# The activation of a gated MLP turned by VectorE and DRAM instead of TensorE, with part of the down projection moved into the next tile

## Chip, cores and metric

One core of a Trainium2 chip runs the kernel. The metric is the device time of one execution in microseconds (us). Before the change three runs gave 551.83 us as median (549.92 to 553.22).

## What is computed

x is 64 x 32 x 512. First comes a long convolution per channel (32 channels, 512 positions) with a mask by length, then a gated MLP with one LoRA adapter per batch element; both are added to x. What the change touches is the second step:

```
gate = lora_add(einsum('bnh,fh->bnf', x, W_gate), x, A_gate, B_gate)
up   = lora_add(einsum('bnh,fh->bnf', x, W_up),   x, A_up,   B_up)
act  = silu(gate) * up                      # F = 1376 columns
down = lora_add(einsum('bnf,hf->bnh', act, W_down), act, A_down, B_down)
x    = x + down
```

lora_add adds 0.5 * (inp @ A[idx].T) @ B[idx].T, with idx chosen per batch element (`itok_B_2_6`). H is 512, the rank 16.

## The kernel before

The first 80 us build the convolution's taps and do the convolution of 16 pairs of channels. The MLP then runs over 16 tiles of 128 rows (4 batch elements x 32 rows), `tiles(...)`: tile 0 alone, a loop of 7 rounds with two tiles each, tile 15 alone. Each engine runs its own `body(a, q, first, last)` with t = 2a + q; semaphores order the engines, and within an engine the order is the one written.

Weights stay in SBUF as pairs, `w_hi`/`w_lo` and `wd_hi`/`wd_lo`, and each product is three matmuls (hi x hi, lo x hi, hi x lo), so that the 32-bit result keeps its digits. The 1376 columns of gate and up are three chunks `CH` of 512, 512 and 352 columns; `BLK` counts them in blocks of 128: 4, 4 and 3 (the last has 96 rows).

TensorE per tile: `base(c, up)` multiplies x by the weights of chunk c (12 matmuls) into `ps_g` or `ps_u`, `lora(c, up)` adds two LoRA matmuls. ScalarE takes SiLU of `ps_g` into `h_act`, VectorE multiplies by `ps_u` (`gated`). The down projection needs the activation with its columns on the partitions, so `transpose_act(c)` (L1035) turns each block of `h_act` on TensorE, against the identity, into `ps_x`. ScalarE casts that into `ht_hi`, VectorE subtracts into `ht_lo` (`ht_hi_part`, `ht_lo_part`), and `down_chunk(c)` (L1044) accumulates in `ps_da` (288 columns) and `ps_db` (224 columns of the output and 64 of the LoRA A product). Chunk 2 is written out at the end of the body, `ps_db` first, since td_m needs it. `lora_a(t)` (L986) makes the next tile's LoRA A product. The LoRA part of the down projection (`transpose_td`, `down_lora`) comes inside the next tile, and so does `finish`, which adds the residual.

SyncE issues every DMA, in one queue: `load_b` (B of a chunk, four issues), `load_a`, `load_bd`, `store` of the output, and index reads ahead of them. The residual itself already takes the road that the change uses for the activation: `square_x` (L816) transposes 32x32 blocks on VectorE into `x_sq`, `store_x` (L324) writes it to the DRAM tensor `xrow` in four issues, one for each 32 partitions, and `load_y` (L328) reads it back turned. `b_raw` are two tiles of 64 partitions; `b_hi_part` and `b_lo_part` (L494, L822) split it into the halves of `b_spl`. GpSimd's `body` (L429, L410) copies the next tile's x and A once A has landed.

## Time and profile before

| | |
|---|---|
| median of three runs | 551.83 us |
| the profiled execution | 551.96 us |
| its span on the core | 550.2 us |
| granted TensorE clock | 0.992 of full |
| TensorE matmul busy | 514.0 us (93%) |
| VectorE busy | 265.1 us (48%) |
| ScalarE busy | 190.9 us (35%) |
| GpSimd busy | 39.2 us (7%) |
| DMA engines, the one queue of SyncE | 39.3% |

Busy time is the sum of an engine's instructions; the span runs from the first to the last record. The time of the execution is 1.8 us longer than its span. Of the views named below, the chain follows the last instruction back to what released it; the timeline lists instructions in order; SPq is SyncE's queue, whose entries are the issues of DMAs and not the transfers.

### The profile page before, as it was taken

To read this page: it belongs to the slowest core of one execution; us is meant where nothing else is said; L and a number is where in the kernel's file an instruction comes from. 1 tells how busy PE (TensorE), PEld (TensorE's weight loads), DVE (VectorE), ACT (ScalarE), POOL (GpSimd) and SP (SyncE) were. 2 spreads that over 40 slices of the span, in tenths; PEclk is the share of its full clock that TensorE was granted. 3 is DMA by queue.
4 is the path that set the end of the run, shared out by engine and by line. 5 is a ranking of instruction groups with operands and counts; after the bars stand their busy time and mean duration, and the time that the engine had idled before them with its cause. 6 is when DMAs were issued, how large, how long until landed. Compare 5 with 4: busy or idle time off the path is not lost.

```text
span 550.2 us, 10109 instructions
## 1 busy us (share of the span) xinstructions
PE 514.0 (93%) x3105; PEld 467.3 (85%) x3105; DVE 265.1 (48%) x572; ACT 190.9 (35%) x411; POOL 39.2 (7%) x55
## 2 busy tenths in 40 slices
PE   0198889999999999999999999999999999999997
PEld 0097787989898989999898989898989898999986
DVE  7882266754444435353445453444444443525342
ACT  6790007333333333242324232323333333324221
POOL 1006700100000000000000000000000000000000
PEclk9998899999999999999999999999999999999999
DMA  7899993423142323242323232322324132423200
GB/s 277 287 344 390 312 331 72 101 71 94 48 108 43 112 51 112 51 112 51 112 48 105 55 97 60 82 67 75 84 51 106 43 110 49 112 51 112 52 21 19
DMA packets 68403, 61.59 MB, mean 112 GB/s; under 512 B 41634, under 2 KB 50242, under 8 KB 68386
## 3 DMA queue, kind: packets, MB, share of 16 engines
q1 hardware_dynamic: 68386, 61.39, 39.3%
q8 instruction: 8, 0.13, 0.1%
q14 instruction: 9, 0.07, 0.0%
HBM read 52.89 MB, written 8.47 MB: 112 GB/s over the span
## 4 chain that ended last, share of the span: by engine, by line
PE 86%; DVE 5%; DMA 5%; ACT 1%; issue 1%; SPq 0%; DVEq 0%
PE ps_g L1006 21%; PE ps_u L1006 21%; PE ps_db L1044 13%; PE ps_da L1044 13%; PE ps_x L1035 3%; PE ps_x L986 3%; PE ps_g L960 3%; DMA toep<-kpad 2%; DMA kpad<-k_sb 2%; PE ps_u L960 2%; PE ps_g L1016 2%; PE ps_u L1016 2%; PE ps_g L1017 2%; PE ps_u L1017 2%; PE ps_da L1104 1%
## 5 line engine op out<-in xcount | busy, mean ns | idle before, releaser
L494 ACT CAST b_spl<-b_raw 64x512 fp32r<-64x512 f32 (+1 forms) x96 | 54.4, 569 | 98.3 <-PE ps_u L1017 78.9
L822 DVE TENSOR_TENSOR b_spl<-b_raw,b_spl 64x512 fp32r<-64x512 f32 (+1 forms) x96 | 60.7, 633 | 53.8 <-ACT b_spl L494 50.1
L1006 PE MATMUL ps_g<-w_hi,x_hi 128*128 128x512 f32 (+1 forms) x192 | 72.7, 379 | 1.4 <-DVE x_lo L917 1.4
L1006 PE MATMUL ps_u<-w_hi,x_hi 128*128 128x512 f32 (+1 forms) x192 | 71.4, 372 | 0.0
L1006 PE MATMUL ps_u<-w_lo,x_hi 128*128 128x512 f32 (+1 forms) x192 | 71.3, 371 | 0.0
L1006 PE MATMUL ps_u<-w_hi,x_lo 128*128 128x512 f32 (+1 forms) x192 | 71.3, 371 | 0.0
L1006 PE MATMUL ps_g<-w_lo,x_hi 128*128 128x512 f32 (+1 forms) x192 | 71.1, 370 | 0.0
L1006 PE MATMUL ps_g<-w_hi,x_lo 128*128 128x512 f32 (+1 forms) x192 | 71.0, 370 | 0.0
L858 DVE TENSOR_TENSOR h_act<-h_act,ps_u 128x512 f32<-128x512 f32 (+1 forms) x48 | 30.3, 632 | 53.7 <-PE ps_u L1017 53.6
L1044 PE MATMUL ps_da<-wd_hi,ht_hi 128*128 128x288 f32 (+1 forms) x176 | 54.5, 310 | 0.2 <-DVE ht_lo L865 0.2
L1044 PE MATMUL ps_db<-wd_hi,ht_hi 128*128 128x288 f32 (+1 forms) x176 | 53.3, 303 | 0.0
L1044 PE MATMUL ps_db<-wd_hi,ht_lo 128*128 128x288 f32 (+1 forms) x176 | 52.1, 296 | 0.0
L1044 PE MATMUL ps_db<-wd_lo,ht_hi 128*128 128x288 f32 (+1 forms) x176 | 52.0, 295 | 0.0
L1044 PE MATMUL ps_da<-wd_lo,ht_hi 128*128 128x288 f32 (+1 forms) x176 | 51.9, 295 | 0.0
L1044 PE MATMUL ps_da<-wd_hi,ht_lo 128*128 128x288 f32 (+1 forms) x176 | 51.7, 294 | 0.0
L517 ACT ACTIVATE h_act<-ps_g 128x512 f32<-128x512 f32 (+1 forms) x48 | 26.5, 552 | 63.8 <-PE ps_g L1017 63.8
L1006 PEld LDWEIGHTS ps_u<-w_hi,x_lo 128*128 128x128 f32 x192 | 36.1, 188 | 5.8
L1006 PEld LDWEIGHTS ps_u<-w_hi,x_hi 128*128 128x128 f32 x192 | 36.1, 188 | 5.7
L1006 PEld LDWEIGHTS ps_g<-w_hi,x_hi 128*128 128x128 f32 x192 | 36.1, 188 | 5.7 <-issue 1.5
L1006 PEld LDWEIGHTS ps_u<-w_lo,x_hi 128*128 128x128 f32 x192 | 36.1, 188 | 5.7
L1006 PEld LDWEIGHTS ps_g<-w_hi,x_lo 128*128 128x128 f32 x192 | 36.0, 188 | 5.7
L1006 PEld LDWEIGHTS ps_g<-w_lo,x_hi 128*128 128x128 f32 x192 | 36.2, 188 | 4.4
(165 smaller groups left out, 871.3 us busy)
## 6 DMA issues: line engine op xcount, KB each, us to landing
a_raw<-atab SPq DMA_DIRECT2D x64, 152.0 KB, 2.4
toep<-kpad SPq DMA_DIRECT2D x16, 512.0 KB, 7.5
b_raw<-btab SPq DMA_DIRECT2D x128, 64.0 KB, 2.0
um<-xr SPq DMA_DIRECT2D x16, 256.0 KB, 5.5
x<-xT SPq DMA_DIRECT2D x8, 512.0 KB, 6.9
w_raw<-wgu SPq DMA_DIRECT2D x8, 512.0 KB, 9.3
xrow<-x_sq SPq DMA_DIRECT2D x64, 64.0 KB, 2.2
y_sb<-xrow SPq DMA_DIRECT2D x16, 256.0 KB, 2.6
```

Of the source, the lines that this page charges most:

```text
L494: nc.scalar.copy(b_spl[0:LR, up, 0:w], b_raw[slot][:, up * w:(up + 1) * w]).then_inc(b_hi, 1)
L517: nc.scalar.activation(h_act[:, s, 0:w], ps_g[s][:, 0:w], ACT.Silu).then_inc(silu_ok, 1)
L822: V.tensor_tensor(b_spl[LR:P, up, 0:w], b_raw[slot][:, up * w:(up + 1) * w], b_spl[0:LR, up, 0:w].bitcast(F32), ALU.subtract).then_inc(b_l ...
L858: V.tensor_tensor(h_act[:, s, 0:w], h_act[:, s, 0:w], ps_u[s][:, 0:w], ALU.mult).then_inc(act_ok, 1)
L960: last = T.matmul(ps_c[slot][:, at + d * NB:at + KB * NB], toep[:, slot, h, d * P:(d + 1) * P], v, start=(d == 0), stop=(d == KB - 1))
L986: ins = T.matmul(ps_x[0][:, 0:P], w, xt[:, kb, :], start=(kb == 0), stop=(kb == KB - 1))
L1006: T.matmul(ps[:, 0:w], xs[:, kb, :], ws[:, kb, col:col + w], start=(kb == 0 and xs is x_hi and ws is w_hi), stop=False)
L1016: T.matmul(ps[:, 0:w], t_hi[:, up, :], b_spl[:, up, 0:w], start=False, stop=False)
L1017: T.matmul(ps[:, 0:w], t_lo[:, up, :], b_spl[:, up, 0:w], start=False, stop=True).then_inc(u_ps if up else g_ps, 1)
L1035: ins = T.transpose(ps_x[bank][0:rows, f * P:(f + 1) * P], h_act[:, s, f * P:f * P + rows], ident[:, :])
L1044: ins = T.matmul(ps[:, 0:c1 - c0], hs[0:rows, f, :], ws[0:rows, f, c0:c1], start=(f == 0 and hs is ht_hi and ws is wd_hi), stop=(bank == 1 ...
L1104: T.matmul(ps_da[:, 0:DA_W], ts[:, :], bd_spl[:, 0:DA_W], start=False, stop=end)
```

## The change

Three things are changed.

- `transpose_act` is gone. `square_h(c)` transposes the 32x32 blocks of `h_act` on VectorE, into a new tile `h_sq` for chunks 0 and 2 and into `x_sq` for chunk 1. `store_h` writes it to a DRAM tensor `hrow` with four issues per chunk, `load_h` reads it back turned into `h_raw` (two tiles; chunk 2 has two issues, since its last block has 96 rows). `ht_hi_part` and `ht_lo_part` now read `h_raw` in SBUF instead of `ps_x`.
- On TensorE only down chunk 0 stays at the end of the tile. `down_rest(t)` does chunks 1 and 2 behind the first gate group of the next tile; in tile 15 it follows at once.
- The orders of SyncE, ScalarE and VectorE follow from that. `load_a` of the next tile comes before the output store. `h_act` has one slot where it had two; the two `b_raw` tiles are now the halves of one tile of 128 partitions, and the halves of `b_spl` swap with them. `lora(0, 0)` comes behind `base(0, 1)` and `down_lora` behind `base(1, 0)`.

```diff
@@ sync
+            def store_h(t, c):
+                col, w = CH[c]
+                sp.wait_ge(hsq_ok, NC * t + c + 1)
+                for part in range(P // Q):
+                    rows = x_sq if c == 1 else h_sq
+                    src = rows[part * Q:(part + 1) * Q, 0:w].rearrange("q (f t) -> q f t", t=Q)
+                    into = bass.AP(tensor=hrow, offset=col * P + part * Q, ap=[[P, Q], [Q * P, w // Q], [1, Q]])
+                    sp.dma_start(into, src).then_inc(h_out, 16)
+
+            def load_h(t, c):
+                f0, nf = BLK[c]
+                full = nf if c < NC - 1 else nf - 1
+                sp.wait_ge(h_out, 16 * (P // Q) * (NC * t + c + 1))
+                src = bass.AP(tensor=hrow, offset=f0 * P * P, ap=[[P, P], [P * P, full], [1, P]])
+                sp.dma_start(h_raw[c % 2][:, 0:full, :], src).then_inc(h_in[c], 16)
...
                 if not last:
                     ids = indices(na, nq)
+                    load_a(na, nq, ids)
+                store_h(t, 0)
+                if not last:
                     load_b(na, nq, 0, ids)
                 if not first:
                     store(*((a, 0) if q == 1 else (a - 1, 1)))
+                load_h(t, 0)
                 if not last:
-                    load_a(na, nq, ids)
                     load_bd(na, nq, ids)
+                store_h(t, 1)
+                if not last:
                     load_b(na, nq, 1, ids)
+                load_h(t, 1)
+                store_h(t, 2)
+                if not last:
                     store_x(t + 1)
+                load_h(t, 2)
+                if not last:
                     load_y(t + 1, nq)
@@ scalar
-                    td_hi_part(t - 1)
+                    ht_hi_part(t - 1, 2)
...
-                    wait(act, ht_ps, n - 1)
+                    wait(act, hsq_ok, n)
...
-                ht_hi_part(0)
+                ht_hi_part(t, 0)
                 silu(2)
                 if not last:
+                    x_hi_part(na, nq, False)
                     b_hi_part(na, nq, 0, 0)
                     b_hi_part(na, nq, 0, 1)
-                ht_hi_part(1)
-                if not last:
-                    x_hi_part(na, nq, False)
-                ht_hi_part(2)
+                ht_hi_part(t, 1)
+                if last:
+                    ht_hi_part(t, 2)
@@ vector
-                    td_lo_part(t - 1)
+                    ht_lo_part(t - 1, 2)
+                    td_m_part(t - 1)
...
+                def square_h(c):
+                    n = NC * t + c
+                    dve.wait_ge(act_ok, n + 1)
+                    if c == 1:
+                        dve.wait_ge(xrow_out, 16 * (P // Q) * (t + 1))
+                    else:
+                        wait(dve, h_out, 16 * (P // Q) * (n - c // 2))
+                        wait(dve, htlo_ok, (NC + 1) * t + c // 2)
+                    V.transpose((x_sq if c == 1 else h_sq)[:, 0:CH[c][1]], h_act[:, 0:CH[c][1]]).then_inc(hsq_ok, 1)
...
+                if not first:
+                    td_lo_part(t - 1)
+                gated(0)
+                square_h(0)
                 b_lo_part(a, q, 1, 0)
-                gated(0)
@@ tensor
+            def down_rest(t):
+                pe.wait_ge(htlo_ok, (NC + 1) * t + 2)
+                down_chunk(1)
+                pe.wait_ge(htlo_ok, (NC + 1) * (t + 1))
+                for f in range(BLK[2][0], FB):
+                    ins = down(f, 1)
+                ins.then_inc(ad_ps, 1)
+                for f in range(BLK[2][0], FB):
+                    ins = down(f, 0)
+                ins.then_inc(down_ps, 1)
...
-                transpose_act(1)
-
-                pe.wait_ge(htlo_ok, (NC + 1) * t + 1)
...
+                pe.wait_ge(htlo_ok, (NC + 1) * t + 1)
                 down_chunk(0)
-                transpose_act(2)
-                pe.wait_ge(htlo_ok, (NC + 1) * t + 2)
-                down_chunk(1)
-                if not last:
+                if last:
+                    down_rest(t)
+                else:
                     lora_a(t + 1)
```

Where instructions move is shown at three places, all in the tile of the loop with q = 1. TensorE before, from the end of down chunk 1 of a tile (ps_da and ps_db) through the LoRA A product to chunk 2:

```order
457 L1044 MATMUL ps_db<-wd_hi,ht_lo 128x288
458 L981 REGISTER_ALU
459 L982 REGISTER_ALU [waits ag_ok]
460 L986 MATMUL ps_x<-xt,a_gu 128x128 [waits htlo_ok,xt_ok]
461 L986 MATMUL ps_x<-xt,a_gu 128x128 x3
462 L1087 REGISTER_ALU
463 L1044 MATMUL ps_db<-wd_hi,ht_hi 128x288 [waits htlo_ok]
```

TensorE after, behind down chunk 0; the first gate group of the next tile (425 to 436) stands ahead of down chunk 1 (438 on):

```order
418 L1042 MATMUL ps_db<-wd_hi,ht_lo 128x288
419 L1029 REGISTER_ALU
420 L1030 REGISTER_ALU [waits ag_ok]
421 L1034 MATMUL ps_x<-xt,a_gu 128x128 [waits tm_ok,xt_ok]
422 L1034 MATMUL ps_x<-xt,a_gu 128x128 x3
423 L1075 ISA
424 L192 ISA [waits xlo_ok]
425 L1080 MATMUL ps_g<-w_hi,x_hi 128x512 [waits act_ok]
...
436 L1080 MATMUL ps_g<-w_hi,x_lo 128x512
437 L1053 ISA
438 L1042 MATMUL ps_da<-wd_hi,ht_hi 128x288 [waits htlo_ok]
```

Down chunks 1 and 2 moved behind twelve matmuls of the next tile, and no transpose stands between them. SyncE's queue before, at the end of a tile, from B's last issue to the residual:

```order
213 L311 DMA b_raw<-btab 16x1024
214 L320 REGISTER_ALU
215 L324 DMA xrow<-x_sq 128x4x32 [waits xsq_ok]
216 L324 DMA xrow<-x_sq 128x4x32 x3
217 L327 REGISTER_ALU
218 L328 DMA y_sb<-xrow 128x512 [waits xrow_out]
```

SyncE's queue after, at the same place:

```order
230 L318 DMA b_raw<-btab 16x1024
231 L369 REGISTER_ALU
232 L371 DMA h_raw<-hrow 128x4x128 [waits h_out]
233 L359 REGISTER_ALU
234 L364 DMA hrow<-h_sq 32x11x32 [waits hsq_ok]
235 L364 DMA hrow<-h_sq 32x11x32 x3
236 L327 REGISTER_ALU
237 L331 DMA xrow<-x_sq 128x4x32 [waits xsq_ok]
238 L331 DMA xrow<-x_sq 128x4x32 x3
239 L369 REGISTER_ALU
240 L371 DMA h_raw<-hrow 128x2x128 [waits h_out]
241 L373 DMA h_raw<-hrow 96x128
```

The load of chunk 1, four stores of chunk 2 and its two load issues are new here; the load of chunk 2 stands behind all four stores of xrow. VectorE after, from the gating of chunk 0 on:

```order
180 L908 TENSOR_TENSOR h_act<-h_act,ps_u 128x512 [waits u_ps,silu_ok]
181 L192 REGISTER_ALU [waits act_ok]
182 L918 STREAM_TRANSPOSE h_sq<-h_act 128x512 [waits htlo_ok,h_out]
183 L853 ISA
184 L854 TENSOR_TENSOR b_spl<-b_raw,b_spl 64x512 [waits b_hi]
185 L853 REGISTER_ALU
186 L854 TENSOR_TENSOR b_spl<-b_raw,b_spl 64x512 [waits b_hi]
187 L864 ISA [waits y_ps]
```

and before, at the same place:

```order
177 L821 ISA
178 L822 TENSOR_TENSOR b_spl<-b_raw,b_spl 64x512 [waits b_hi]
179 L858 TENSOR_TENSOR h_act<-h_act,ps_u 128x512 [waits u_ps,silu_ok]
180 L821 REGISTER_ALU
181 L822 TENSOR_TENSOR b_spl<-b_raw,b_spl 64x512 [waits b_hi]
182 L832 ISA [waits y_ps]
183 L833 TENSOR_TENSOR y_sb<-y_sb,ps_da 128x288 [waits y_in]
184 L834 TENSOR_TENSOR y_sb<-y_sb,ps_db 128x224
```

The gating stood between the two splits of B; now it and the transpose stand ahead of both.

## Rows read from the trace of the kernel before

**Rows 1.** The page: busy us, share and instructions of each engine; the chain by engine.

```profile
PE 514.0 (93%) x3105; PEld 467.3 (85%) x3105; DVE 265.1 (48%) x572; ACT 190.9 (35%) x411; POOL 39.2 (7%) x55
...
PE 86%; DVE 5%; DMA 5%; ACT 1%; issue 1%; SPq 0%; DVEq 0%
```

**Rows 2.** The chain in order of time, one tile: start us, us, what.

```profile
343.54 2.79 PE ps_g L1006 x12
346.90 2.80 PE ps_u L1006 x12
350.64 2.80 PE ps_g L1006 x12
...
357.15 0.44 PE ps_x L1035 x4
...
359.83 1.92 PE ps_u L1006 x12
362.08 0.44 PE ps_x L1035 x4
369.23 0.89 PE ps_x L986 x8
...
372.52 2.79 PE ps_g L1006 x12
```

**Rows 3.** Timeline of TensorE, chunk 2's transposes: start, us, engine, line, what.

```profile
336.56 0.49 PE L1035 MATMUL ps_x<-ident,h_act 128*128 128x128 f32 x3
...
337.02 0.29 PE L1044 MATMUL ps_da<-wd_lo,ht_hi 128*128 128x288 f32 x1
```

**Rows 4.** SyncE's queue: its timeline over one tile, and the second index reads.

```profile
311.73 0.35 SPq L328 DMA_DIRECT2D y_sb<-xrow  x1
314.65 1.85 SPq L311 DMA_DIRECT2D b_raw<-btab  x4
...
322.86 1.81 SPq L311 DMA_DIRECT2D b_raw<-btab  x4
324.95 0.38 SPq L333 DMA_DIRECT2D out<-y_sb  x1
325.56 1.91 SPq L270 DMA_DIRECT2D a_raw<-atab  x4
327.65 1.84 SPq L317 DMA_DIRECT2D bd_raw<-btab  x4
...
336.44 2.64 SPq L324 DMA_DIRECT2D xrow<-x_sq  x4
...
L262 SPq FUSED_REGOPS  x8: 46/106/152, 316.5 to 318.8; - x8
```

**Rows 5.** Issue durations (ns, min/median/max) of two lines; landings of xrow's and y_sb's transfers.

```profile
L247 SPq DMA_DIRECT2D kpad<-k_sb x4: 326/341/971, 20.5 to 42.3; - x4
...
L253 SPq DMA_DIRECT2D toep<-kpad x16: 377/384/469, 22.1 to 69.8; - x16
...
xrow<-x_sq SPq DMA_DIRECT2D x64, 64.0 KB, 2.2
...
DMA to landing us min/median/max: 2.6/2.6/2.8
```

The last line is that of y_sb<-xrow (L328), the one before gives KB and the median landing.

**Rows 6.** VectorE's block transpose, and the two splits of the turned chunk 2.

```profile
L816 DVE STREAM_TRANSPOSE x_sq<-xt x16: 704/704/709, 80.1 to 509.6; 128x512 f32<-128x512 f32 x16
...
337.08 0.37 ACT L529 CAST ht_hi<-ps_x 128x256 fp32r<-128x256 f32 x1 [2.33 <-PE ps_x L1035]
...
337.99 0.28 DVE L869 TENSOR_TENSOR ht_lo<-ps_x,ht_hi 96x128 fp32r<-96x128 f32 x1
```

**Rows 7.** Timeline of TensorE in tile 0, down chunk 0.

```profile
101.38 0.40 PE L1044 MATMUL ps_da<-wd_hi,ht_hi 128*128 128x288 f32 x1 [0.22 <-DVE ht_lo L865]
```

**Rows 8.** Timeline of the last tile: VectorE's gating of chunk 1, TensorE's down chunk 2.

```profile
531.18 0.69 DVE L858 TENSOR_TENSOR h_act<-h_act,ps_u 128x512 f32<-128x512 f32 x1 [1.81 <-PE ps_u L1017]
...
542.99 0.29 PE L1044 MATMUL ps_db<-wd_hi,ht_hi 128*128 128x288 f32 x1
```

176 lines of the change are left out of this document (77 added, 99 removed).

## The prediction

> **What bounds the kernel now.** I read the busy shares first: TensorE is busy for 93% of the span and carries 86% of the chain that ended last [rows 1]; VectorE, ScalarE and the DMA engines are busy less than half of it. The second view is the chain in order of time. From the first gate product of one tile to that of the next it is TensorE alone, 372.52 - 343.54 = 28.98 us, and nothing in it is a wait [rows 2]; sixteen such tiles are 464 of the 550 us. So in the middle tiles every instruction taken off TensorE shortens the kernel by its own length, as long as no other engine or queue then comes last. The third view is SyncE's queue [rows 4], because the change puts its new transfers there: whether the gain arrives is decided on that queue.
>
> **What is removed.** Eleven transposes per tile on TensorE. Four are 0.44 us in the chain, twice (357.15 and 362.08) [rows 2]. The three of chunk 2 stand between 336.56 and 337.02 [rows 3]: the start of the second matmul behind them comes 0.46 us after their own, of which 0.13 is the pitch of one 288-column matmul (18 of them fill the 2.40 from 370.12 to 372.52 in the chain), so 0.33. Sum 1.21 us per tile. TensorE's own work becomes 28.98 - 1.21 = 27.8 us.
>
> **What is added, and what covers it.** I count from the moment Z at which the up projection of chunk 0 is complete. Behind it come on TensorE the lengths of [rows 2]: 2.8 (chunk 1's gate), 0.48 (the LoRA part of the down projection of the tile before) and 0.46 (one LoRA pair; both together are the 0.94 between 346.90 + 2.80 and 350.64), 2.8, 0.46 and 2 x (1.92 + 0.32) for chunk 2 (359.83 to 362.08 is 2.25). Chunk 1 is therefore complete at Z + 7.0 and chunk 2 at Z + 11.5. Then follow down chunk 0 (24 matmuls at 0.133 = 3.2), the LoRA A product (0.89 at 369.23), the next tile's first gate group (2.8), down chunk 1 (3.2) and down chunk 2 (2.4, from 370.12 to 372.52). So the turned chunk 0 is needed at Z + 11.3, chunk 1 at Z + 18.2, chunk 2 at Z + 21.4.
>
> The new road of a chunk is: gating multiply (0.69 at 531.18 [rows 8]; about 0.5 for chunk 2's 352 columns), 32x32 block transpose, four stores to DRAM, a load back, the cast on ScalarE and the subtraction on VectorE. The transpose exists: 0.704 us for 128x512 [rows 6]; for 352 columns I scale it to 0.5. VectorE and ScalarE are idle for half the time, so these add no length by themselves, only latency. A store issued as xrow's lands 2.2 us after its issue, a load as y_sb's 2.6 (2.8 at most) [rows 5].
>
> The unknown is the time that SyncE needs to issue one hrow store; the trace has two rows for it. xrow's store takes 0.66 us with its gap (2.64 for four [rows 4]). kpad's takes 0.341 (median of four) [rows 5]. They differ in kind: xrow's store walks its tile as 32x16x32 and DRAM as 128x4x32, while kpad's has one shape on both sides, 32x8x16, and toep's load with one shape, 128x2x512, is issued in 0.384. The hrow store is 32x16x32 on both sides. I take 0.38 with its gap, and keep 0.66 as the other end. A load of h_raw I put at 0.4.
>
> SyncE's order behind Z, with the lengths of [rows 4]: hrow store of chunk 0 from Z + 1.7 (gating and transpose end there), 1.5; B of the next tile 2.0; the output store 0.6; load of chunk 0 0.4; bd 2.1; this is Z + 8.3, the square of chunk 1 is there at Z + 8.6; store 1.5, B 2.0, load 0.4: Z + 12.5, the square of chunk 2 is there at Z + 12.7; store 1.5 (Z + 14.2); xrow's four stores 2.65 (Z + 16.9); load of chunk 2, two issues, the second from Z + 17.3.
>
> - Chunk 0: load issued at Z + 5.8, landed 8.4, ScalarE 0.6 and VectorE 0.7: Z + 9.8, needed at 11.3. Margin 1.5 us.
> - Chunk 1: load at Z + 12.1, landed 14.7, behind it ScalarE's and VectorE's turn (VectorE has the next tile's x and B ahead of it until 15.5): Z + 16.6, needed at 18.2. Margin 1.6 us.
> - Chunk 2: landed at Z + 19.3 to 19.9; from the first ScalarE cast to the end of the last subtraction 1.2 us (337.08 to 338.27 [rows 6]): Z + 20.6 to 21.2, needed at 21.4. **Margin 0.2 to 0.8 us**, the thinnest of the three.
>
> SyncE's own round must also fit in 27.8 us. Behind the load of chunk 2: 0.9 waiting for xrow to land, 0.36 for y_sb, 0.3 for the loop, the first four index reads 2.6 (312.08 to 314.65), B of chunk 2 1.85, the second four 2.5 (from 316.5), A 2.1 [rows 4]. Together 10.6, plus 15.4 from the list above: 26.0 us. It fits, with 1.8 to spare. The A load is no longer behind the output store; it waits for the subtraction of wd_lo, which comes some 2 us ahead of Z, so it starts at Z - 1.6 and is out at Z + 0.5, ahead of the first hrow store at 1.7. GpSimd waits only for that A load, and now gets it earlier.
>
> A new order costs nothing at two more places. VectorE now gates and transposes chunk 0 before chunk 1's first B split: the split is ready at Z + 2.4, TensorE wants it at Z + 3.1. The single h_act tile makes the next SiLU wait for the transpose, which is done at 1.7 where the next SiLU comes at about 3.9.
>
> **The two ends.** In tile 0 VectorE is loaded with weight remainders, and TensorE already waits there for ht_lo (101.38) [rows 7]. The transpose of chunk 0 (0.7, ahead of the split) and that of chunk 1 (0.7, ahead of the last remainders) push both, so TensorE starts down chunk 0 at about 102.25 and not 101.38; of the tile's transposes only the last 0.33 come off behind that point. Tile 0: +0.5. In the last tile no next gate group covers the road. Chunk 1: gated from 531.18 [rows 8], square ready at 532.6, stores to 534.2, landed 536.05, load landed 538.8, ready 540.1, while TensorE is there at 538.6: 1.6 us. Chunk 2: its store follows the load of chunk 1 (536.8), landed 540.1, load landed 542.7, ready 544.1; TensorE, at 543.3 by then, loses 0.8. Down chunk 2 began at 542.99 [rows 8] and now begins at about 544.2: +1.2 net of the transposes.
>
> **Sum.** Against the profiled run's own 551.96 (span 550.2 and 1.8 around it; the three plain runs have a median of 551.83, so the two agree): 14 middle tiles x 1.21 = -16.9, tile 0 +0.5, last tile +1.2. 551.96 - 15.2 = 536.8 us.
>
> **Rivals.**
> 1. *SyncE's queue becomes the bound, and the kernel is slower.* If the hrow store is issued at xrow's 0.66, twelve of them cost 3.4 us more per tile. The load of chunk 2 then ends at Z + 20.5 and not 17.1, and the ring closes: behind that last issue landing, cast, subtraction and down chunk 2 take 5.7 us, then 3.8 us of TensorE to the next Z and 1.7 to the next hrow store, 11.2 in all, plus 18.8 of issues: 30.0 us per tile against 28.98. 14 x 1.06 + 3 at the ends gives 570 us; with chunk 2's 11-block stores at 11/16 of the price 29.2 and 558. It decides from a mean of about 0.57 per store on (a tile of 28.98); below about 0.45 TensorE stays the bound. For it: xrow's row is the only one with as many 128-byte runs (512). Against: the equal shapes. The Trainium skill (DMA: Bandwidth & Descriptors, "Issuing engines are not separate DMA queues") calls issue time "usually small relative to the DMA itself", which speaks against this rival; the trace does not agree, four xrow issues (2.64 us) are longer than one landing (2.2).
> 2. *The round trip of chunk 2 is later than its margin.* Behind xrow's stores and beside B and A loads the landing may be 0.5 to 1 us longer than 2.6. Each us beyond the margin is 14 us of kernel: 0.5 gives 544, 1.0 gives 551. For it: the margin of 0.2 to 0.8. Against: all sixteen landings of y_sb, which are issued right behind xrow's stores, are between 2.6 and 2.8 [rows 5]. The Trainium skill (VectorE: DVE Perf Modes, "The three transpose paths") warns of a transpose by strided plain copy as 19 times slower where the innermost destination stride is large, and sends 128x128 blocks to TensorE. Its condition is not met here, the innermost run is 32 contiguous floats, and xrow's row, turned the same way, shows 2.2 us for 64 KB.
> 3. *No change.* A price of 0.54 to 0.6 per store gives back just what the transposes gave: 549 to 555.
>
> **Chances.** Forecast (TensorE stays the bound, 533 to 541) 0.62; rival 2, 541 to 549, 0.15; rival 3 and the mild half of it, 549 to 555, 0.07; rival 1, 0.12; below 533, 0.04. The range takes the forecast and rival 2: 533 to 550. This kernel's measurement tells 0.5% from no change; by that bound faster has 0.80, same 0.07, slower 0.13.
>
> **What would show it.** Right: the first gate products of two tiles 27.8 us apart, no wait of TensorE for ht_lo in the middle tiles, hrow<-h_sq at about 0.34 us per issue, SyncE waiting for VectorE's square once or twice per tile. Wrong: hrow stores at 0.6 us and TensorE waiting at the first matmul of down chunk 2 in every tile (rival 1), or that wait with cheap issues and landings of 3 us and more (rival 2). A wait at chunk 1 or 0, or at B's first split, would say that my order of VectorE's work is wrong.

## The result, and the profile after

The changed kernel is slower: 576.56 us (median of 6 runs, 574.11 to 580.70) against 551.53 (6 runs, 549.92 to 553.22), a ratio of 1.046 (95% interval 1.042 to 1.050). The prediction was 536.8, faster. The profiled execution took 580.7 us with a span of 578.9, against 551.96 and 550.2. It is the longest of the six.

The page of the changed kernel: the busy lines answer to the first of [rows 1], the chain line to the second.

```profile
PE 510.6 (88%) x2929; PEld 458.5 (79%) x2929; DVE 297.4 (51%) x620; ACT 196.5 (34%) x411; POOL 43.3 (7%) x55
...
SPq 42%; PE 25%; DMA 12%; issue 10%; DVE 8%; ACT 3%; DVEq 0%
SPq L364 15%; SPq L318 9%; PE ps_u L1080 8%; SPq L331 7%; DMA h_raw<-hrow 6%; PE ps_db L1042 4%; SPq L324 4%; PE ps_da L1042 4%; SPq L371 4%; PE ps_g L1008 3%; DMA toep<-kpad 2%; PE ps_u L1008 2%; DVE h_sq L918 2%; DVE h_act L908 2%; DMA kp
```

The 176 transposes are gone (3105 to 2929 matmuls), yet TensorE's share of the chain fell from 86% to 25%, and SyncE's queue has 42%, with the hrow stores (L364) first. The next view is the list of waits (engine, line, releaser: us in total, times, longest us).

```profile
PE ps_db L1042 <- DVE ht_lo L875: 23.9, 15, 2.1
...
PE ps_da L1042 <- DVE ht_lo L872: 6.9, 5, 4.2
```

TensorE waits in each of the 15 tiles that have a predecessor, for the last piece of the chunk 2 before it, 1.6 us on average, and one wait of 4.2 us, for chunk 0, lies in tile 0. A middle tile in SyncE's timeline, then what follows it on ScalarE, VectorE and TensorE (start us, us, engine, line, what); the rows of before are [rows 4].

```profile
342.55 1.97 SPq L364 DMA_DIRECT2D hrow<-h_sq  x4
344.80 1.85 SPq L318 DMA_DIRECT2D b_raw<-btab  x4
346.95 0.38 SPq L340 DMA_DIRECT2D out<-y_sb  x1
347.47 0.39 SPq L371 DMA_DIRECT2D h_raw<-hrow  x1
348.13 1.86 SPq L324 DMA_DIRECT2D bd_raw<-btab  x4
350.03 2.05 SPq L364 DMA_DIRECT2D hrow<-x_sq  x4
352.36 1.85 SPq L318 DMA_DIRECT2D b_raw<-btab  x4
354.32 0.39 SPq L371 DMA_DIRECT2D h_raw<-hrow  x1
354.82 2.02 SPq L364 DMA_DIRECT2D hrow<-h_sq  x4
356.95 2.65 SPq L331 DMA_DIRECT2D xrow<-x_sq  x4
359.72 0.55 SPq L371 DMA_DIRECT2D h_raw<-hrow  x1
360.31 0.48 SPq L373 DMA_DIRECT2D h_raw<-hrow  x1
```

```profile
362.73 0.40 ACT L540 CAST ht_hi<-h_raw 128x256 fp32r<-128x256 f32 x1 [2.26 <-DMA h_raw<-hrow]
...
363.70 0.28 DVE L875 TENSOR_TENSOR ht_lo<-h_raw,ht_hi 96x128 fp32r<-96x128 f32 x1
...
364.04 0.40 PE L1042 MATMUL ps_db<-wd_hi,ht_hi 128*128 128x288 f32 x1 [1.67 <-DVE ht_lo L875]
```

Chunk 0's up projection is complete at Z = 340.83 here. The first hrow store goes out at Z + 1.7, as predicted; the second h_raw issue of chunk 2 at Z + 19.5 instead of 17.3. TensorE stands at Z + 21.6 (predicted 21.4) and gets the data at Z + 23.2.

A second thing was in no part of the prediction. The windows around that wait (us; busy us of PE, PEld, DVE, ACT, POOL; granted clock, DMA share, GB/s):

```profile
339.50:362.40 22.90, 22.87 (x134) 20.49 (x132) 13.17 (x25) 8.54 (x18) 1.38 (x2) 1.00 0.64 141
362.40:364.04 1.64, 0.00 (x1) 0.00 (x1) 0.62 (x2) 0.60 (x2) 0.00 (x0) 1.00 0.43 145
364.04:365.50 1.46, 1.46 (x11) 1.46 (x12) 0.00 (x0) 0.00 (x0) 0.00 (x0) 1.00 0.00 0
365.50:367.50 2.00, 2.00 (x11) 2.00 (x10) 0.29 (x1) 0.00 (x0) 0.00 (x0) 0.51 0.33 76
367.50:369.50 2.00, 2.00 (x8) 1.55 (x7) 0.89 (x1) 0.78 (x1) 0.00 (x0) 0.64 0.04 14
```

TensorE stood still for 1.64 us, worked for 1.5, and then had a granted clock of 0.51, its lower level of 1.2 GHz, for some 3 us, though it was busy all the time. Five of the 14 middle tiles have a mean clock of 0.95 and last 31.35 us or more; the others, at 1.00, last 29.39 to 29.75. In the kernel before, every tile shows 1.00. The number of such tiles differs between executions: the profiled one has a mean granted clock of 0.978, four of the other five have 0.984. One stretch at 0.50 for some 3 us lowers the mean over 579 us by about 0.003, so by this estimate those four had about two stretches fewer.

**Where the 43.9 us between predicted and measured span went** (535.0 and 578.9), by the starts of the transposes of td (one per tile; 28.99 apart in the kernel before): the first comes at 124.32, 7.8 us later than in a kernel with only the moved down projection (experiment 1), where I had 0.5 for the tile (7.3 us); the next 14 steps take 426.3 us instead of 14 x 27.82 = 389.5 (36.8 us, of which 14 x 1.79 = 25.1 is the step of 29.61, the mean of the nine ordinary tiles, and 11.7 the rest of the five longer tiles with their low clock; the first two of them, at 33.0 and 32.5, also have longer and further waits); the last tile is 0.9 us longer, 0.3 less than predicted.

### The profile page after: what moved, and what is told of

It reads as the page before. It is cut to its first block, busy times and chain, and to the rows that moved or that the text cites. A ratio compares the mean times of both kernels' runs of the same rounds, so it can differ in the third digit from the quotient of the medians.

```text
span 578.9 us, 10207 instructions
## 1 busy us (share of the span) xinstructions
PE 510.6 (88%) x2929; PEld 458.5 (79%) x2929; DVE 297.4 (51%) x620; ACT 196.5 (34%) x411; POOL 43.3 (7%) x55
## 2 busy tenths in 40 slices
DMA packets 182579, 84.15 MB, mean 145 GB/s; under 512 B 133794, under 2 KB 164418, under 8 KB 182562
## 4 chain that ended last, share of the span: by engine, by line
SPq 42%; PE 25%; DMA 12%; issue 10%; DVE 8%; ACT 3%; DVEq 0%
SPq L364 15%; SPq L318 9%; PE ps_u L1080 8%; SPq L331 7%; DMA h_raw<-hrow 6%; PE ps_db L1042 4%; SPq L324 4%; PE ps_da L1042 4%; SPq L371 4%; PE ps_g L1008 3%; DMA toep<-kpad 2%; PE ps_u L1008 2%; DVE h_sq L918 2%; DVE h_act L908 2%; DMA kpad<-k_sb 2%
## 5 line engine op out<-in xcount | busy, mean ns | idle before, releaser
L1042 PE MATMUL ps_db<-wd_hi,ht_hi 128*128 128x288 f32 (+1 forms) x176 | 54.5, 310 | 23.9 <-DVE ht_lo L875 23.9
L1080 PE MATMUL ps_u<-w_hi,x_hi 128*128 128x512 f32 (+1 forms) x192 | 72.7, 378 | 0.0
L540 ACT CAST ht_hi<-h_raw 128x512 fp32r<-128x512 f32 (+1 forms) x48 | 26.3, 548 | 135.8 <-DMA h_raw<-hrow 135.8
L872 DVE TENSOR_TENSOR ht_lo<-h_raw,ht_hi 128x512 fp32r<-128x512 f32 (+1 forms) x48 | 29.0, 603 | 81.6 <-ACT ht_hi L540 51.0
L528 ACT CAST b_spl<-b_raw 64x512 fp32r<-64x512 f32 (+1 forms) x96 | 51.7, 571 | 53.3 <-PE ps_u L1091 33.6
L1042 PEld LDWEIGHTS ps_db<-wd_hi,ht_hi 128*128 128x128 f32 (+1 forms) x176 | 33.6, 191 | 27.7 <-DVE ht_lo L875 27.7
L1042 PE MATMUL ps_da<-wd_hi,ht_lo 128*128 128x288 f32 (+1 forms) x176 | 53.9, 306 | 0.0
L1042 PE MATMUL ps_da<-wd_lo,ht_hi 128*128 128x288 f32 (+1 forms) x176 | 53.9, 306 | 0.0
L463 POOL COPY xt<-x 128x512 f32 (+1 forms) x15 | 11.5, 766 | 435.9 <-DMA a_raw<-atab 435.9
L1042 PEld LDWEIGHTS ps_da<-wd_hi,ht_hi 128*128 128x128 f32 (+1 forms) x176 | 35.0, 199 | 9.9 <-DVE ht_lo L872 4.7
```

What stands on the lines that cost most here:

```text
L528: nc.scalar.copy(b_spl[b_rows(slot), up, 0:w], b_raw[b_rows(slot), up * w:(up + 1) * w]).then_inc(b_hi, 1)
L540: nc.scalar.copy(ht_hi[:, f0:f0 + full, :], raw[:, 0:full, :]).then_inc(hthi_ok, 1)
L872: V.tensor_tensor(ht_lo[:, f0:f0 + full, :], raw[:, 0:full, :], ht_hi[:, f0:f0 + full, :].bitcast(F32), ALU.subtract).then_inc(htlo_ok, 1)
L1042: ins = T.matmul(ps[:, 0:c1 - c0], hs[0:rows, f, :], ws[0:rows, f, c0:c1], start=(f == 0 and hs is ht_hi and ws is wd_hi), stop=(bank == 1 ...
L1080: T.matmul(ps[:, 0:w], xs[:, kb, :], ws[:, kb, col:col + w], start=(kb == 0 and xs is x_hi and ws is w_hi), stop=False)
```

## The experiments

Each ratio is against executions of the kernel before that belong to the same experiment; "step" is the mean distance of two td transposes over the 14 middle tiles of the profiled execution.

| | kernel | median us | ratio (95%) | step us |
|---|---|---|---|---|
| | before | 551.53 | | 28.99 |
| | after | 576.56 | 1.046 (1.042 to 1.050) | 30.45 |
| 1 | move only | 551.87 | 1.000 (0.998 to 1.003) | 29.03 |
| 2 | traffic only | 558.04 | 1.012 (1.007 to 1.016) | 29.25 |
| 3 | stall, 5 transposes | 552.79 | 1.003 (1.000 to 1.005) | 28.99 |
| 5 | stall, 8 transposes | 586.33 | 1.063 (1.060 to 1.067) | 31.12 |
| 4 | xrow from ScalarE | 566.68 | 1.028 (1.023 to 1.033) | 29.67 |
| 6 | xrow behind h_raw | 571.80 | 1.038 (1.035 to 1.042) | 30.08 |
| 13 | xrow in blocks | 560.64 | 1.017 (1.015 to 1.018) | 29.15 |
| 14 | hrow from ScalarE | 555.22 | 1.009 (1.005 to 1.012) | 28.94 |
| 7 | tile 0's order | 575.83 | 1.043 (1.038 to 1.047) | 30.36 |
| 8 | reordered | 551.04 | 1.000 (0.998 to 1.003) | 28.77 |
| 9 | round shortened | 550.71 | 0.999 (0.997 to 1.001) | 28.61 |
| 10 | 9, xrow in blocks | 551.38 | 1.001 (0.998 to 1.004) | 28.77 |
| 11 | h_raw 0 before a | 569.51 | 1.033 (1.030 to 1.036) | 29.98 |
| 12 | 11, tile 0 changed | 570.48 | 1.034 (1.032 to 1.037) | 30.11 |
| 15 | third order | 557.97 | 1.012 (1.008 to 1.016) | 29.23 |
| 16 | 15, bd last | 540.09 | 0.981 (0.978 to 0.983) | 28.06 |

### The two parts of the change apart (1, 2)

```diff
@@ tensor, on the kernel before (1)
                 base(0, 0)
-                if not first:
-                    transpose_td(t - 1)
+                down_rest(t - 1)        # chunks 1 and 2
+                base(0, 1)
+                transpose_td(t - 1)
...
                 transpose_act(2)
-                pe.wait_ge(htlo_ok, (NC + 1) * t + 2)
-                down_chunk(1)
@@ sync, on the kernel before (2)
+                store_h(t, 0)           # source: w_lo, a constant tile
...
+                load_h(t, 0)            # nobody reads h_raw
```

> The kernel before with the second part of the change alone: the activation is still turned by TensorE (11 transposes per tile), and only the down projection of chunks 1 and 2 moves behind the next tile's first gate group. Nothing goes through DRAM. Theory A (the ring: SyncE's issues between the first hrow store and chunk 2's h_raw load, the landing and the casts decide when chunk 2's rows are ready, TensorE waits 1.7 us for them in every tile, and the clock falls behind some of those waits): without the round trip nothing is late, TensorE keeps its 28.99 us per tile, total 549 to 554 us. Rival B (the new order on TensorE, with silu and the gating product further apart, is itself what costs): 1 us or more per tile, 565 us or more.

> The kernel before, with the changed kernel's DMA work added and used by nobody: the same 12 hrow stores and 4 h_raw loads per tile on SyncE in the changed kernel's order, the stores taking their data from a constant tile instead of the turned activation (so hrow holds nothing of use); b_raw's two slots lie in one tile, as in the changed kernel, to make room. The products are still computed from TensorE's own transposes. Theory A: the traffic (84 MB instead of 62) costs TensorE nothing by itself, since no TensorE instruction waits for it; SyncE is busy in 28 us of a tile and TensorE's loads have slack, so 550 to 556 us. Rival C (SyncE's issue time or the DMA engines are the bound: a, b or y arrive late): 29.5 us per tile or more, 560 us or more, with TensorE waiting for b_spl or for lora_a's operands.

The move alone costs nothing that shows in the total; it is 29.03 us per tile against 28.99, with no wait. Rival B falls. With the traffic alone (84.15 MB instead of 61.59) TensorE's busy time and clock stay at those of before, 511.8 us and 1.00, and eight of the 14 steps are 28.97 to 29.01 us; but the total is 1.2% up, more than theory A allowed. The profiled execution, at 555.18 us, is the fastest of four (the others took 557.8 to 559.2), so the profile shows only a part of this. The largest part that it shows is one tile of 30.87 us:

```profile
193.72 0.55 PE L1074 MATMUL ps_x<-ident,h_act 128*128 128x128 f32 x3 [1.69 <-DVE ht_lo L904]
```

That wait is of the experiment's own making: so that the unused tile is not written twice at a time, ScalarE waits for h_raw's landing before the third SiLU, up to 5.2 us. So 1.2% holds the cost of the traffic and of this added wait together, and how it divides was not measured. `load_a` stands here behind the load of chunk 0, as it does not in the changed kernel.

### A wait on TensorE without the traffic (3, 5)

```diff
@@ vector, on the kernel before
+                for _i in range(NPAD):        # 5 in run 3, 8 in run 5
+                    V.transpose(pad_sq[:, :], w_lo[:, 0, 0:512])
                 ht_lo_part(2)
```

> The kernel before with five added VectorE square transposes of a constant tile (0.7 us each, one waiting for the other, some 4.5 us) ahead of chunk 2's ht_lo, which TensorE waits for; nothing of the computation is left out. In the profile of before that ht_lo is ready 2.5 us before TensorE wants it, so TensorE should wait about 2.0 us per tile at the down projection of chunk 2, with no added DMA. Theory A on the clock (a wait of this length on TensorE is enough for stretches at half clock to follow): windows of the trace with the granted clock well below 1.00 right behind some of the waits, and a total above 551.5 + 16 x 2.0 = 583 us by some microseconds. Rival D (the half clock of the changed kernel comes from its DMA traffic or its longer run, not from the wait): granted clock 1.00 all through the tiles as in before, total 580 to 585 us.

> The kernel before with eight added VectorE square transposes of a constant tile ahead of chunk 2's ht_lo instead of the five of the last stall run, whose 3.65 us ended 0.4 us before TensorE wanted the result and made no wait; nothing of the computation is left out. Three more at 0.73 us put chunk 2's ht_lo 1.7 to 1.9 us behind TensorE's wish in each of 16 tiles, with no added DMA: about the wait of the changed kernel. Theory A on the clock (such a wait is enough for stretches at half clock to follow behind some of them): granted clock well below 1.00 in windows behind some waits, tiles of 32 us or more among those of 30.8, total 585 us or more. Rival D (the half clock of the changed kernel comes with its DMA traffic): clock 1.00 all through, every tile 30.7 to 30.9 us, total 578 to 582 us.

Five transposes missed their purpose: 3.65 us of them filled a gap of VectorE and the margin behind it, and TensorE never waited. Eight made a wait of 1.65 us, the size of that in the changed kernel. Twelve of the 14 steps are 30.88 to 30.91 us, two are 32.44 and 32.45, with a mean clock of 0.95. The timeline and the windows of one of these two:

```profile
455.95 0.40 PE L1053 MATMUL ps_db<-wd_hi,ht_hi 128*128 128x288 f32 x1 [1.65 <-DVE ht_lo L875]
...
450.00:455.00 5.00, 4.30 (x34) 4.11 (x32) 4.76 (x8) 0.53 (x2) 0.00 (x0) 1.00 0.36 59
...
457.00:459.00 2.00, 2.00 (x13) 2.00 (x12) 0.49 (x2) 0.94 (x4) 0.00 (x0) 0.64 0.27 66
459.00:461.00 2.00, 2.00 (x7) 1.61 (x7) 1.15 (x4) 0.24 (x1) 0.00 (x0) 0.50 0.11 24
```

The same fall to the lower level comes behind a wait, with no hrow traffic at all: rival D falls, and theory A holds. The extra price is 1.55 us per tile that is hit, and about the same in the changed kernel: its three shorter hit tiles take 31.35 to 31.54 us against 29.61, 1.7 to 1.9 more, of which their longer waits (1.67 to 1.89 us against 1.52) are 0.15 to 0.37. Why two tiles are hit here and five in the changed kernel is not explained by these runs.

### What sets the wait for chunk 2: SyncE's issues or the landing (4, 6, 13, 14)

```diff
@@ changed kernel (4): scalar
                     b_hi_part(na, nq, 0, 1)
+                    store_x(t + 1)          # on ScalarE's queue, gone from SyncE
                 ht_hi_part(t, 1)
@@ changed kernel (6): sync
-                    store_x(t + 1)
                 load_h(t, 2)
+                    store_x(t + 1)          # load_y in the next tile, behind load_a
@@ changed kernel (13): store_x
-                    src = x_sq[...].rearrange("q (k j p) -> q k j p", p=Q, k=KB)
+                    src = x_sq[...].rearrange("q (f p) -> q f p", p=Q)
@@ changed kernel (14): scalar
                 b_hi_part(a, q, 1, 1)
+                store_h(t, 0)               # 1 ahead of ht_hi_part(t, 0), 2 behind the next b
```

> The changed kernel with the next tile's four xrow stores (2.65 us of issuing per tile) given to ScalarE's queue, behind its b_spl casts, where it idles from 354.06 to 357.51; all else as in the changed kernel. Theory A (ring): chunk 2's h_raw loads are issued about 2.2 us earlier after the first hrow store of the tile, the rows are ready just before TensorE wants them (362.4 in the tile shown), the wait is gone and with it the half clock: 27.8 to 28.2 us per tile, total 538 to 548 us, tile 0 still about 9 us late. Rival E (the stores of two engines go through the same hardware and slow each other, or the landing gets longer): the hrow burst of chunk 2 takes over 3 us instead of 2.0 and the wait stays, 570 us or more.

> The changed kernel with the xrow stores behind chunk 2's h_raw load on SyncE (y_sb's load then stands in the next tile behind load_a); all on SyncE as before. The run with xrow on ScalarE's queue had shown the same distance from chunk 2's first hrow store to its h_raw load as the changed kernel (4.86 and 4.90 us) though SyncE had nothing to issue in between: what takes that time would be the landing of hrow beside the xrow packets, not SyncE. Theory F (the landing of hrow, 1.8 to 2.0 us alone and some 3.2 beside an xrow burst, is the term): h_raw is issued 3.8 to 4.1 us after the first hrow store of chunk 2, the wait at chunk 2 falls from 1.67 to 0.7 to 0.9, 28.7 to 28.9 us per tile, total 553 to 565 us with less of the half clock. Rival G (the landing of hrow takes 3 us there with or without xrow beside it): the distance stays 4.6 or more and the total 570 us or more. Rival H (SyncE has no room at the tile's end: the xrow stores push the next tile's b and a loads and its first hrow store): the first hrow store comes 1 us or more behind its square, and the gain is given back.

> The changed kernel with xrow kept in hrow's block layout (one shape on both sides of the store), y_sb read back block by block; nothing else. The four xrow issues between chunk 2's hrow stores and its h_raw load then take some 2.0 us instead of 2.65. Issue theory (the prediction's way of adding: the ring is the sum of SyncE's issues): chunk 2's h_raw load comes 0.65 us earlier after its first hrow store (4.25 instead of 4.90 us), the wait falls by 0.65, total 563 to 567 us with fewer stretches at half clock. Landing theory F (the distance is hrow's landing, 3.2 us beside xrow's packets against 1.4 to 1.5 when nothing follows): the distance stays at 4.6 to 4.9 and the total within 3 us of the changed kernel's 576.5.

> The changed kernel with the hrow stores of all three chunks issued by ScalarE (chunk 0 behind b_spl's casts, chunk 1 ahead of chunk 0's ht_hi, chunk 2 behind the next b_spl casts), h_raw, xrow and all else still on SyncE in the same order. SyncE's round falls by 6 us. Issue theory: 27.8 to 28.2 us per tile, total 540 to 550 us. Landing theory F, with ScalarE in order as a rival of its own: ScalarE waits for each square before it goes on (chunk 1's square is done 8 us after the up projection of chunk 0, and silu of chunk 2 stands behind the burst of 2 us), so chunk 0's and chunk 1's casts get later while chunk 2's hrow still lands beside xrow's packets: a wait of 0.5 to 1.5 us per tile stays, total 555 to 575 us.

The measure is the distance from chunk 2's first hrow store to its h_raw load in SyncE's timeline. It is 4.90 us in the changed kernel (354.82 to 359.72 above). Runs 4, 6 and 13, in this order:

```profile
346.72 2.95 ACTq L537 DMA_DIRECT2D xrow<-x_sq  x4
346.76 2.08 SPq L364 DMA_DIRECT2D hrow<-h_sq  x4
351.62 0.38 SPq L371 DMA_DIRECT2D h_raw<-hrow  x1
```

```profile
348.65 1.98 SPq L364 DMA_DIRECT2D hrow<-h_sq  x4
352.04 0.38 SPq L371 DMA_DIRECT2D h_raw<-hrow  x1
```

```profile
312.67 2.02 SPq L365 DMA_DIRECT2D hrow<-h_sq  x4
314.79 2.04 SPq L331 DMA_DIRECT2D xrow<-x_sq  x4
316.95 0.44 SPq L372 DMA_DIRECT2D h_raw<-hrow  x1
```

- Run 13 takes 0.6 us off the four xrow issues (2.65 to 2.04); y_sb is read back block by block, behind chunk 2's load, and nothing else changes. The distance falls to 4.28, the wait from 1.52 us on average in the ordinary tiles to 0.84 in those behind the first three, the total by 16 us. The issue theory had 4.25 for the distance. Its total of 563 to 567 was too high: besides 14 times the shorter wait, tile 0 is 3.7 us shorter (first td transpose at 120.62) and no tile has the low clock. Theory F, as I had put it after run 4, falls: with all stores on one queue the last issue sets the time.
- Run 6 has nothing between the two: 3.39 us, that is 1.4 us of landing behind the end of the burst. Run 4 has nothing between them on SyncE either, but ScalarE's queue issues xrow at the same moment: 4.86 us, 2.8 behind the burst. The landing of hrow doubles beside another queue's stores, and it takes back what the freed SyncE gave at this place. TensorE's wait still falls, to 0.7 to 1.0 us in most tiles, since the h_raw loads of chunk 2 are landed 2.3 to 2.5 us after the first of the two issues, against 2.6 to 3.0 in the changed kernel. Run 4's total, 566.68 us, lies between both its theories. The Trainium skill (DMA: Bandwidth & Descriptors, "Issuing engines are not separate DMA queues") says that transfers issued by different engines run on the same 16 DMA engines and interleave. The trace agrees: 2.8 us behind the burst against 1.4.
- In run 6 the wait for chunk 2 is all but gone (0.17 us), and rival H has come: the first hrow store of a tile goes out at 306.42 though its square ended at 304.17. SyncE had no 2.65 us to give at the tile's end, and TensorE waits 2.44 us for chunk 0 instead in this tile, 0 to 2.3 us in the other middle tiles.
- Run 14 frees SyncE of 6 us per tile and gets 28.94, not 27.8. ScalarE is in order: its cast of chunk 0 stands behind its own burst for chunk 1.

```profile
332.77 1.95 ACTq L528 DMA_DIRECT2D hrow<-x_sq  x4
334.89 0.62 ACT L536 CAST ht_hi<-h_raw 128x512 fp32r<-128x512 f32 x1 [3.26 <-issue]
```

The chunk had landed at 333.24. TensorE then waits 0.7 to 0.9 us for chunk 0 in every middle tile. The bound moved to the engine that took the issues.

### Tile 0 (7)

```diff
@@ changed kernel, sync, tile 0 alone
+                    store_h(t, 0)
                     ids = indices(na, nq)
+                    load_h(t, 0)
                     load_a(na, nq, ids)
-                    store_h(t, 0)
```

> The changed kernel with another order of SyncE's issues in tile 0 alone: chunk 0's hrow stores ahead of the index reads and of load_a, chunk 1's ahead of the next tile's b. In the changed kernel tile 0's first hrow store is issued at 97.36 though its square is done at 92.86, and TensorE waits 4.24 us for chunk 0's ht_lo at 106.39. Theory A: the store goes out near 93, ht_lo of chunk 0 is ready about 5 us earlier, the first transpose of td is at 117 to 119 instead of 124.3, the later tiles are unchanged at 29.6, total 567 to 572 us. Rival: VectorE's and ScalarE's preparation of the weights sets tile 0's end (they hold the casts of wd between the squares), under 2 us is gained, 574 us or more.

The store does go out at 90.66 and the wait for chunk 0 falls from 4.24 to 1.22 us, but a new one of 5.55 us stands at chunk 2, whose h_raw load is issued only at 112.85, behind the next tile's b and xrow. First td transpose at 124.00 against 124.32: nothing gained, neither theory's number. In run 16 only bd's issues stand in tile 0 between chunk 2's hrow stores and its load, xrow is on ScalarE's queue, and the transpose is at 116.53.

### Reordering until no wait is left (8 to 12, 15, 16)

Run 8 takes xrow to ScalarE's queue behind chunk 2's casts, in the next tile, where no hrow is under way, and puts hrow and h_raw of chunks 1 and 2 directly one behind the other. The later runs change SyncE's order, and the index reads as said below:

```diff
@@ sync, a middle tile, b of chunk 2 and the index reads ahead of it
-8:  a, y_sb, hrow 0, b, out, h_raw 0, bd, hrow 1, h_raw 1, hrow 2, h_raw 2, b
+9:  hrow 0, a, h_raw 0, b, out, hrow 1, y_sb, bd, h_raw 1, hrow 2, h_raw 2, b
+11: hrow 0, h_raw 0, a, b, hrow 1, out, y_sb, bd, h_raw 1, hrow 2, h_raw 2, b
+15: hrow 0, h_raw 0, a, y_sb, out, hrow 1, b, h_raw 1, hrow 2, bd, h_raw 2, b
+16: hrow 0, y_sb, out, h_raw 0, a, hrow 1, b, h_raw 1, hrow 2, h_raw 2, bd, b
```

Run 9 also reads a tile's indices once instead of twice in every second tile; 11 to 16 keep that. Run 10 is 9 with xrow in blocks, run 12 is 11 with one VectorE pair swapped in tile 0.

> The changed kernel with all of it put right that the traces point to: the xrow stores on ScalarE's queue in the next tile behind chunk 2's casts (y_sb's load behind load_a), on SyncE hrow and h_raw of chunks 1 and 2 directly one behind the other and the next b after them, and tile 0 with its hrow stores first. Theory F: hrow of chunk 2 goes out about 1.2 us earlier and lands alone; its rows are ready within 0.3 us of TensorE's wish, 27.8 to 28.1 us per tile, tile 0 about 2 to 4 us behind that of before, granted clock 1.00: total 532 to 542 us. Rival G (the landings stay at 3 us): a wait of 0.5 to 1 us per tile, 28.4 to 28.8, total 545 to 553 us. Rival I (the half clock has a cause of its own): tiles of over 30 us remain though no wait is left.

> The reordered kernel of the last call with SyncE's round put right: the first hrow store of a tile goes ahead of load_a and y_sb's load (there it went out at 352.60 behind a_raw at 350.07, 0.95 us behind the end of its square at 351.65), the h_raw load of chunk 0 ahead of the next b, and the indices of a tile are read once instead of twice in every second tile and in tile 0 (a read of four takes some 2.4 us of SyncE's time). Theory J (in the reordered kernel SyncE's round of some 28.8 us is the bound, so that every second tile waits at chunk 0): no wait is left in the later tiles, 27.8 to 28.0 us per tile, total 535 to 542 us. Rival K (what is left is landing time: chunk 0's hrow and h_raw come late beside the a and b loads whatever the order): 28.4 us per tile or more, 546 us or more.

> The last kernel with xrow kept in hrow's layout (blocks of 128 tokens by 128 columns, so that the two sides of a store have one shape) and y_sb read back block by block; the xrow store then reads as the hrow stores do, some 0.50 us each instead of 0.66 to 0.74 on ScalarE's queue. Theory J: nothing on the path, since ScalarE's burst lies where nobody waits: within 1.5 us of the last kernel. Rival: y_sb's load in pieces of 512 bytes lengthens the landings beside it, 2 us or more slower.

> The kernel with the shortened round, with chunk 0's h_raw load put ahead of load_a (SyncE then waits some 1.5 us for hrow's landing), and the out store and y_sb's load behind chunk 1's hrow stores. In the last kernel the h_raw load of chunk 0 was issued at 354.54 behind a_raw's four and its rows reached ScalarE only at 358.73, 4.2 us later against 2.0 alone, and TensorE waited up to 0.67 us for chunk 0. Theory L (a landing is as long as the bytes issued just before it make it): the landing of chunk 0's h_raw falls to 2.0 to 2.6 us, no wait is left at chunk 0, 28.05 to 28.2 us per tile (that is 29.03 less the 0.96 us that TensorE's transposes really took), total 541 to 546 us. Rival M (SyncE's wait for the landing costs its round: chunk 1 or 2 is late instead, or the first hrow store): 28.4 us per tile or more, 549 us or more.

> The same, and in tile 0 alone VectorE makes chunk 1's b_spl of gate ahead of the square of chunk 0 (in all versions with the square in front TensorE waited 1.55 us there, 0.57 in the kernel before). Theory: the wait at 91.4 falls to some 0.85 us, but the wait of 1.2 us for chunk 0's ht_lo behind the last wd pieces takes the gain: within 0.5 us of the last kernel. Rival: 0.7 us are gained, a tenth of a per cent, at the edge of what can be told.

> The kernel with the shortened round in a third order of SyncE's issues: hrow 0, h_raw 0, a, y_sb, out, hrow 1 (at its square's end, 7.0 us after hrow 0), the next b, h_raw 1, hrow 2, bd, h_raw 2, b. In the last order chunk 1's hrow went out 1.4 us behind its square and its h_raw load stood behind bd, and VectorE waited 2.2 us for y_sb's landing. If the waits are a matter of order: chunk 0's rows arrive as in the last kernel (no wait), chunk 1's some 15.3 us after the first hrow store where TensorE wants them at 16.3, no wait is left, 28.1 to 28.3 us per tile, 541 to 547 us. If the landings grow with what is issued beside them whatever the order (a and b loads of 0.6 and 0.26 MB lie in every gap): one of the three chunks stays 0.3 to 0.7 us late, 28.5 us per tile or more, 549 us or more.

> The kernel of e15 with bd's loads behind chunk 2's h_raw load, and y_sb's load and the out store between chunk 0's hrow stores and its h_raw load. If order decides: the distance from hrow 2 to h_raw 2 falls from 4.11 to 3.4 us, the wait of 0.7 us per tile at chunk 2 is gone or below 0.2, 28.2 to 28.4 us per tile, total 545 to 550 us, at or just below the kernel before. If the landings grow with what lies beside them in any order: 28.8 us per tile or more, 555 us or more.

Runs 8 and 9 give back all that the change had lost and no more. Both theories that promised 532 to 542 fell short; the totals are in the ranges of rivals G and K. In 9 the h_raw load of chunk 0 goes out at 354.54 behind a_raw's four issues, ScalarE gets it at 358.73, 4.2 us later, and TensorE waits 0.2 to 0.7 us for chunk 0. Run 11 put the load first, and the landing fell to 2.8 us, but hrow of chunk 1 now went out 1.4 us behind its square and its h_raw stood behind bd: a wait of 1.0 to 1.6 us at chunk 1 from the third middle tile on, rival M, 569.5 us. Runs 10 and 12 changed nothing that can be told, as both said.

Run 15 sends hrow 1 at its square's end. A wait of 0.4 to 1.0 us was left at chunk 2, with bd's four issues between its hrow and its h_raw (4.11 us apart), and 557.97 us is the number of its second theory, growing landings. Run 16 moves bd away, and y_sb and out into SyncE's wait for hrow 0:

```profile
317.50 1.97 SPq L364 DMA_DIRECT2D hrow<-h_sq  x4
319.58 0.44 SPq L335 DMA_DIRECT2D y_sb<-xrow  x1
320.29 0.37 SPq L340 DMA_DIRECT2D out<-y_sb  x1
320.96 0.38 SPq L371 DMA_DIRECT2D h_raw<-hrow  x1
321.58 1.97 SPq L277 DMA_DIRECT2D a_raw<-atab  x4
324.35 1.93 SPq L364 DMA_DIRECT2D hrow<-x_sq  x4
326.56 1.85 SPq L318 DMA_DIRECT2D b_raw<-btab  x4
328.52 0.39 SPq L371 DMA_DIRECT2D h_raw<-hrow  x1
329.02 1.99 SPq L364 DMA_DIRECT2D hrow<-h_sq  x4
332.58 0.38 SPq L371 DMA_DIRECT2D h_raw<-hrow  x1
```

The hrow bursts still take 1.93 to 1.99 us, but chunk 2's and its load are 3.56 us apart where they were 4.90. TensorE's td transposes, and the page's lines of this kernel:

```profile
314.47 0.27 PE L1146 MATMUL ps_x<-ident,td_m 128*128 128x128 f32 x1
...
342.29 0.27 PE L1146 MATMUL ps_x<-ident,td_m 128*128 128x128 f32 x1
```

```profile
PE 494.1 (92%) x2929; PEld 446.0 (83%) x2929; DVE 294.7 (55%) x620; ACT 197.3 (37%) x411; POOL 39.1 (7%) x55
...
PE 72%; DMA 10%; SPq 8%; DVE 5%; issue 3%; ACT 2%; DVEq 0%; ACTq 0%
```

27.82 or 27.83 us per tile in nine of the 14 middle steps, where the prediction had 27.8, and 540.09 us in all: 1.9% faster than the kernel before, 6.3% faster than the changed kernel. The transfers and the block transposes are the same; besides the order, ScalarE issues xrow's stores and some index reads are gone. Against the 29.03 of run 1, the new order on TensorE with its transposes, 27.82 is 1.21 us less, the sum that the prediction gave for the transposes, and not the 0.96 of run 11's text. The total lies 5 us below run 16's own forecast of 545 to 550. Which of run 16's two moves (bd, or y_sb and out) did more was not tried apart. The distance of hrow 2 and h_raw 2 fell by 0.55 to 0.66 us, about the size of the wait that went, which speaks for bd. Its rival's price, 28.8 us per tile in any order, falls. Landings do differ with the order: chunk 0's load takes 3.9 to 4.8 us to land in the middle tiles of run 16, behind y_sb's load and the output store (320.96 above, and ScalarE's cast only at 325.14), and 2.7 to 3.0 in run 15, where nothing is issued between hrow and it. In run 16 TensorE does not wait for it in nine of the 14 middle steps.

## Why the prediction was wrong

By its own steps:

- **What bounds the kernel, and what the transposes are worth.** Right. 28.98 less 1.21 was given as 27.8; TensorE freed of waits shows 27.82 (run 16).
- **The times at which TensorE wants each chunk.** Right: Z + 21.4 predicted for chunk 2, Z + 21.6 measured.
- **The price of an hrow store: the step that failed first.** I took kpad's 0.34 with a gap, 0.38, for the equal shapes. Four take 1.97, 2.05 and 2.02 us, 0.50 each. The issue durations of this line (ns, min/median/max), where [rows 5] has the rows of before:

```profile
L364 SPq DMA_DIRECT2D hrow<-h_sq x128: 303/480/530, 97.4 to 566.0; - x128
```

The first issue of a burst takes 0.30 to 0.34 us where SyncE has waited ahead of it (chunk 0) and 0.41 to 0.44 right behind other issues; the three behind it take 0.46 to 0.53. kpad's four stores, 20.5 to 42.3 us into the kernel, stood alone, each with its wait: its 0.341 was the price of a first issue. The equal shapes were worth something (0.51 against 0.66 for xrow, run 13) but not what I gave them. Three bursts up to chunk 2's load are 1.5 us over the sum.
- **The rest of SyncE's sum.** Gaps of 0.1 to 0.3 us between the groups, and 0.55 for a load where I had 0.4, are the other 0.7 of the 2.2 us by which the second issue came late. One number in the text said what that meant: a margin of 0.2 to 0.8 us. A margin smaller than the spread of my own price (0.38 to 0.66 over twelve stores, 3.4 us) was no margin, and the chance of 0.62 ignored it.
- **"Below about 0.45 TensorE stays the bound, from 0.57 on the kernel is slower".** The measured price of 0.50 lies between, and the kernel is already slower. The form of rival 1, a ring through SyncE, landing, casts and down chunk 2, is what the profile shows; its thresholds were too kind. At 0.50 its own sum is 30.0 - 12 x 0.16 = 28.1 us, 16.9 of them from the first hrow store to the end of the last h_raw issue and 11.2 behind. Measured are 342.55 to 360.79, 18.2 us, with the gaps and the longer loads in it, and 11.4 behind in a tile at full clock: 29.6. So the ring closed above 28.99 at a price that should have left room. Of the 1.5 us between 28.1 and 29.6, some 0.6 is a slip in the sum itself: the ring ends the load of chunk 2 at Z + 17.1, but the list of issues has its second issue from Z + 17.3 on, which at 0.4 ends at 17.7. The rest is gaps and longer loads. Rival 1 named 570 us, 576.6 were measured.
- **SyncE's round of 26.0 us.** Wrong by more than 2 us. SyncE stands idle ahead of the first hrow store for 0.5 to 1.5 us, 1.0 on average over the ordinary tiles, until VectorE's square is done; so its round does not set the changed kernel's time, but 29.6 less 1.0 is 28.6 us and not 26.0. That is over the 27.8 of TensorE: by this count SyncE could not have kept up in this order of issues even with chunk 2 on time, which no rival said. Run 6 showed it when xrow moved to the tile's end.
- **The two ends.** The last tile came as forecast (+0.9 for +1.2). Tile 0 did not, 7.3 us beyond: I had reckoned with VectorE alone and not with SyncE, which reads indices and issues a_raw ahead of the first hrow store. The square was done at 92.86, the store went out at 97.36. Timelines of SyncE and of TensorE, where [rows 7] has the row of before:

```profile
95.37 1.94 SPq L277 DMA_DIRECT2D a_raw<-atab  x4
97.36 2.05 SPq L364 DMA_DIRECT2D hrow<-h_sq  x4
```

```profile
106.39 0.58 PE L1042 MATMUL ps_da<-wd_hi,ht_hi 128*128 128x288 f32 x1 [4.24 <-DVE ht_lo L872]
```

- **The clock.** A wait was priced at its own length. In some tiles it cost about 1.6 us more, because the granted clock fell behind it (run 5 shows this without any of the change). With five such tiles it is some 8 of the 28.7 us that the profiled execution lost (580.7 against 551.96).
- **Rival 2's landing.** It did not come in the changed kernel. The casts of chunk 2 start 2.4 us behind the second load issue (360.31 to 362.73), inside the 2.0 to 2.6 of the prediction, and end with the last subtraction 1.25 us later (1.2 predicted). The load was issued 2.2 us late and had a margin of 0.2 to 0.8: that leaves 1.4 to 2.0 us, and TensorE waits 1.67. So the issues alone make the wait. The loads of chunks 0 and 1 landed with a median of 2.9 us, inside their larger margins.

## What to carry to other kernels

When a transfer's round trip through one issuing queue gets a margin of a few tenths, the order of that queue is the design: between a store and the load that reads it back nothing should be issued that is longer than the store's landing. Here the kernel took 576.6 us in one order and 540.1 in another, with the same transfers; xrow's stores had moved to a second queue and some index reads were saved. Price an issue by a row that stands in a burst of its own kind, and compare the spread of the price, times the number of issues on the path, with the margin. Before calling a change bad, look whether its gain shows up in the engine's own work; here it did, 1.21 us per tile as forecast.
